# Cross-attention and quantised FFN on one core: the first two mixed tiles split ahead of the query turns, the x rows loaded ahead of the context blocks, row statistics and normalised rows one row tile sooner

## The chip, the cores and the metric

The kernel runs on one NeuronCore of a Trainium2 chip. The metric is device time in microseconds. Five engines work side by side and meet only at semaphores: TensorE (PE; its weight loads are shown as PEld), VectorE (DVE), ScalarE (ACT), GpSimd (POOL) and SyncE (SP), which here issues every DMA, in program order and on one queue. The granted clock of TensorE stands in the profile as a share of full speed: 1.00 is 2.4 GHz, 0.50 is 1.2 GHz.

## The reference

Eight batches of x (512 rows of 512) attend to a context of 512 rows of 512, then a quantised feed-forward net follows. Cut to what matters:

```
def attention(v, k, q, mask, W, b):          # v = k = context, q = layernorm(x)
    scores = einsum('bqd,bkd->bqk', q, k) / sqrt(512)
    att = softmax(where(mask, -1e9, scores))
    atted = swapaxes(einsum('bqk,bkd->bqd', att, v), -1, -2)
    return einsum('bdl,ol->bdo', atted, W) + b
def ffn(x, w_gate, w_up, w_down):            # weights: a scale per row; x and h: one scale each
    h = quant(silu(quant(x) @ quant(w_gate).T) * (quant(x) @ quant(w_up).T))
    return h @ quant(w_down).T
x = x + attention(context, context, layernorm(x), mask, W, b)
x = x + ffn(layernorm(x), ...)
```

One scale for the whole of x and one for the whole of h split the program into three stages with a full barrier between them: attention, gate and up products, down products.

## The kernel before

Everything the change touches is in the attention stage, in which batch n runs from 0 to 7. A 512x512 matrix is held as T = 4 row tiles of 128 partitions by 512 columns. To keep float32 accuracy each operand is held as a high and a low part (`_hi`, `_lo`), and each product is the sum of three matmuls; four column groups k of 12 matmuls make one 512x512 product.

TensorE's order in batch n is `scores(n, k)` (queries by context, k = 0 to 3), `merged(n-1, k)` (the last product of the batch before), `mixed(n, k)` (probabilities by W). All three write the same four PSUM tiles `mm[k]`. So `scores(n+1, k)` may start only when `mm[k]` has been read out: ACT copies it to `g_hi` (`mixed_hi`, L489), DVE makes `g_lo` (`mixed_lo`, L711), which raises `g_ready`. `scores(n+1, k)` also waits for `qT_ready`, the low part of the transposed queries.

The queries of batch n+1 go round a long way. DVE takes row statistics of x (`row_stats1`, L634 to L641), POOL the inverse deviation (`make_rstd1`, L385), DVE the bias (`row_bias1`, L656), ACT writes the normalised rows `qn` (`norm1`, L506). SP stores them to DRAM (`move_q`, L269), waits for the whole store, and loads them back in blocks as `qb` (L275). DVE turns each block (`turn_q`, L651), ACT makes `qT_hi` (`query_hi`, L471), POOL makes `qT_lo` (`query_lo`, L416). The context goes the same way without the store: `load_cb` (L261), `turn_c` (L646), `turned_hi` (L459), `turned_lo` (L410).

SP's DMAs in batch n, in order: transposes of the weights rounded in batch n-1 (`turn_w`, L300 and L304, after ACT's `weights16` L536 and L542), mask n+1 (L282), context rows n (L256), raw weights of batch n (L289, L294, after the transposes have landed), store and reload of the queries of n+1, store of the attention output of n-1 (`store_x1`, L309), context blocks n+2 (`load_cb`), then x of n+2 (`load_x`, L279). `load_x` waits for `x_free`, the landing of that very store, as the three x buffers take turns.

ACT ends a batch with `weights_round` (L524, L528) and `weights16`, which stand behind the four `g_hi`; DVE's `weights_scale` stands ahead of `turn_q`. POOL adds the merge bias to x (`add_bias`, L398). Nothing is scheduled by a planner: the order on each engine is the order of the loops below.

Of the kernel before, what the change touches and what calls it, by code (L numbers as in the profile page):

```python
# [48 lines left out]
def cross_attention_ffn(nc, x, context, mask, w_merge, b_merge, clip_x, clip_down,  # L49
                        w_gate, w_up, w_down, out):  # L50
    B, L, D = x.shape
    I = w_gate.shape[0]
    T = L // P
# [13 lines left out]
    with ExitStack() as whole:  # L67
# [19 lines left out]
        def attention():  # L87
            with ExitStack() as ctx:
# [165 lines left out]
                def _(sp):  # L254
# [23 lines left out]
                    def load_x(n):  # L278
                        sp.dma_start(xs[n % 3][:], x_t[n]).then_inc(x_in[n % 3], 16)  # L279
# [53 lines left out]
                    for n in range(B):  # L333
                        if n:
                            turn_w(n - 1)
                        if n < B - 1:
                            sp.wait_ge(mneg_made, T * (n + 1))
                            load_mask(n + 1)
                        if n:
                            sp.wait_ge(c_ready, T * n)  # L340
                            load_c(n)
                            sp.wait_ge(w_done, through(n - 1, w_turns))
                            load_w(n)
                            if n < B - 1:
                                move_q(n + 1)
                            for t in range(T):
                                store_x1(n - 1, t)
                        if n < B - 2:
                            sp.wait_ge(cT_ready, T * (n + 1))
                            load_cb(n + 2)  # L350
                            if n:
                                sp.wait_ge(min2, T * n)
                                sp.wait_ge(x_free[(n - 1) % 3], 64 * ((n - 1) // 3 + 1))
                            else:
                                sp.wait_ge(wm_done, T)
                            load_x(n + 2)
                        if n % 2:
                            store_scale(n)
                    sp.wait_ge(x_free[0], 64 * len(range(0, B, 3)))
# [10 lines left out]
                @block.gpsimd  # L370
                def _(gp):
                    def first_mneg(t):
                        if t == 0:
                            gp.wait_ge(mask_in, 16)
                        nc.gpsimd.tensor_scalar(mneg[:, t, :], mk[:, t, :], MASKED, None, ALU.mult).then_inc(mneg_made, 1)

                    def first_rstd(k):
                        a, b = FIRST_ROWS[k]
                        gp.wait_ge(var1, k + 1)
                        nc.gpsimd.tensor_tensor(rstd1[:, a:b], ve1[:, a:b], minus_half[:, a:b],  # L380
                                                ALU.pow).then_inc(rstd1_made, 1)

                    def make_rstd1(n):
                        gp.wait_ge(var1, 3 + n)
                        nc.gpsimd.tensor_tensor(rstd1[:], ve1[:], minus_half[:, 0:T], ALU.pow).then_inc(rstd1_made, 1)  # L385

                    def make_rstd2(a, b):
                        gp.wait_ge(var2, 1 if a == 0 else 2)
                        nc.gpsimd.tensor_tensor(ln2[:, a:b, 4 * T:5 * T], ve2[:, a:b, :],
                                                minus_half[:, 0:(b - a) * T].rearrange("p (b t) -> p b t", t=T),  # L390
                                                ALU.pow).then_inc(rstd2_made, 1)

                    def add_bias(n):
                        if n == 0:
                            gp.wait_ge(const_in, 48)
                        for t in range(T):
                            gp.wait_ge(q_ready, T * n + t + 1)
                            nc.gpsimd.tensor_tensor(xs[n % 3][:, t, :], xs[n % 3][:, t, :], bias[:],  # L398
                                                    ALU.add).then_inc(resid_ready, 1)

                    def make_c_lo(n):
                        gp.wait_ge(c_hid, n + 1)
                        for t in range(T):
                            nc.gpsimd.tensor_tensor(c_lo[:, t, :], cx[:, t, :], c_hi[:, t, :].bitcast(F32),  # L404
                                                    ALU.subtract).then_inc(c_ready, 1)

                    def turned_lo(n):
                        for t in range(T):
                            gp.wait_ge(cT_hid, T * (n - 1) + t + 1)
                            nc.gpsimd.tensor_tensor(columns(cT_lo, t), blocks(cb[:, t, :]), columns(cT_hi, t).bitcast(F32),  # L410
                                                    ALU.subtract).then_inc(cT_ready, 1)

                    def query_lo(n):
                        for t in range(T):
                            gp.wait_ge(qT_hid, T * (n - 2) + t + 1)
                            nc.gpsimd.tensor_tensor(columns(qT_lo, t), blocks(qb[:, t, :]), columns(qT_hi, t).bitcast(F32),  # L416
                                                    ALU.subtract).then_inc(qT_ready, 1)

                    nc.gpsimd.memset(minus_half[:], -0.5).then_inc(consts, 1)
                    nc.gpsimd.memset(ident[:], 0.0).then_inc(consts, 1)  # L420
                    gp.wait_ge(consts, 2)
                    nc.gpsimd.affine_select(out=ident[:], in_=ident[:], compare_op=ALU.not_equal, fill=1.0,
                                            base=0, pattern=[[-1, P]], channel_multiplier=1).then_inc(consts, 1)
                    gp.wait_ge(consts, 3)
                    nc.gpsimd.tensor_copy(ident16[:], ident[:]).then_inc(consts, 1)
                    first_rstd(0)
                    first_rstd(1)
                    first_mneg(0)
                    first_rstd(2)
                    for t in range(1, T):  # L430
                        first_mneg(t)
                    for n in range(B):
                        add_bias(n)
                        if n < B - 1:
                            make_rstd1(n + 1)
                            turned_lo(n + 1)
                            if n:
                                query_lo(n + 1)
                        make_c_lo(n)
                    make_rstd2(0, B - 1)  # L440
                    make_rstd2(B - 1, B)
# [3 lines left out]
                def _(act):  # L445
# [106 lines left out]
                    for n in range(B):  # L552
                        last, start = n == B - 1, n == 0
                        for t in range(T):
# [7 lines left out]
                            else:  # L562
                                if t < 2:
                                    make_mneg(n, t + 2)
                                if t:
                                    probs_hi(n, t - 1)
                        if not start:
                            if not last:
                                for t in range(T):
                                    norm1(n + 1, t)  # L570
                            probs_hi(n, T - 1)
                        if not last:
                            for t in range(T):
# [1 line left out]
                                if start:  # L575
                                    norm1(n + 1, t)
                        context_hi(n)
                        if not (start or last):
                            for t in range(T):
                                query_hi(n + 1, t)  # L580
                        for k in range(T):
                            mixed_hi(n, k)
                            if start:
                                for g in Q1_AFTER[k]:
                                    transposed_hi(n + 1, T + g)
                            if not last and k in (1, 2):
                                make_mneg(n + 1, k - 1)
# [9 lines left out]
                def _(dve):  # L597
# [184 lines left out]
                    for n in range(B):  # L782
                        last, start = n == B - 1, n == 0
                        for t in range(T):
                            mask_and_max(n, t)
                            if start:
# [4 lines left out]
                                invert_sum(n, t)  # L791
                                if t < 2:
                                    transposed_lo(0, T + 2 + t)
                            elif t:
                                invert_sum(n, t - 1)
                                if t < 3 and not last:
                                    row_stats1(n + 1, 2 * t - 2, 2 * t)
                                if t == 3 and not last:
                                    row_bias1(n + 1)
                                    for k in range(T // 2):  # L800
                                        turn_c(n + 1, k)
                                probs_lo(n, t - 1)
                        if start:
                            probs_lo(n, T - 1)
                            row_stats1(n + 1, 0, T)
# [12 lines left out]
                                row_stats2(n - 1, k)  # L818
                                row_min2(n - 1, k)
                        weights_scale(n)  # L820
                        if not (start or last):
                            for t in range(T):
                                turn_q(n + 1, t)
                        for k in range(T):
                            if start:
                                mixed_lo(n, k)
                                for g in Q1_AFTER[k]:
# [576 lines left out]
```

## Time and profile before

| | |
|---|---|
| median of 3 runs | 561.69 us (559.78 to 562.91) |
| the profiled execution's own time | 564.96 us |
| its span, first to last instruction | 562.9 us |
| attention stage | 0 to 317.3 us |
| PE busy | 526.2 us (93% of the span) |
| DVE, ACT, POOL busy | 416.4, 311.9, 168.3 us |
| mean granted clock | 0.979 |
| DMA queue, share of 16 engines | 65.7% |

The span is 2.1 us shorter than the profiled execution's own time, which includes what lies around the first and last instruction. The profiled execution is 3.3 us above the median of the timed runs. A busy share is a mean over stages; the stage with the change is read in laps, from the first score matmul of one batch to the first of the next.

### The profile page before, as it was taken

The numbers are of one execution on the slowest core, as the hardware profiler recorded it, in microseconds if no ns is written. First come the engines' busy times: TensorE is split into PE (matmuls) and PEld (weight loads), VectorE is DVE, ScalarE is ACT, GpSimd is POOL, SyncE is SP. The second block draws the span as 40 slices with busy tenths as digits, with TensorE's granted clock in tenths as the row PEclk, the third lists the DMA queues.
The fourth block names the chain that finished last, engine by engine and source line by source line (L and its number), as shares of the span: only waits on it lengthen the run. The fifth ranks groups of instructions, "written<-read, shape, count | busy, mean of one in ns | idle before, by whom it ended". The sixth has DMA issues, their size and how long they took to land. (4 is left out here: it accounts for less than half of the span.)

```text
span 562.9 us, 7193 instructions
## 1 busy us (share of the span) xinstructions
PE 526.2 (93%) x2344; PEld 341.0 (61%) x2344; DVE 416.4 (74%) x791; ACT 311.9 (55%) x456; POOL 168.3 (30%) x142
## 2 busy tenths in 40 slices
PE   5889979979999799896999899999999999999996
PEld 4678768858778588785888544444444444344442
DVE  5686886848868578586483767887787777599985
ACT  4758747477386564973723255455545543877520
POOL 3556347375494553953824000000000000000000
PEclk9989999989999799999999899999999999999999
DMA  8808796897978968996357554596421000779773
GB/s 273 231 3 176 266 236 153 252 245 241 233 173 263 242 203 221 215 268 151 78 167 95 174 172 164 164 318 234 123 71 37 19 19 4 305 270 399 259 276 150
DMA packets 93726, 106.17 MB, mean 189 GB/s; under 512 B 36864, under 2 KB 67584, under 8 KB 91136
## 3 DMA queue, kind: packets, MB, share of 16 engines
q1 hardware_dynamic: 93696, 105.80, 65.7%
q8 instruction: 16, 0.26, 0.2%
q14 instruction: 14, 0.11, 0.1%
HBM read 66.06 MB, written 31.72 MB: 174 GB/s over the span
## 5 line engine op out<-in xcount | busy, mean ns | idle before, releaser
L1325 PE MATMUL gu<-hid,gu_T 128*128 128x512 f16 x704 | 152.1, 379 | 0.0
L1325 PEld LDWEIGHTS gu<-hid,gu_T 128*128 128x128 f16 x704 | 68.8, 98 | 83.3 <-DVE hid L1240 0.4
L1143 ACT ACTIVATE hid<-gu,gu_mul 128x512 f32<-128x512 f32 x88 | 59.5, 685 | 73.6 <-PE gu L1325 68.0
L1221 DVE SCALAR_TENSOR_TENSOR hid<-gu,gu_mul,hid 128x512 f32 (+1 forms) x88 | 65.0, 746 | 33.4 <-PE gu L1325 29.5
L881 PE MATMUL mm<-cT_hi,qT_hi 128*128 128x512 f32 x128 | 54.4, 425 | 19.8 <-DVE g_lo L711 18.1
L1366 PE MATMUL gu<-wd_T,gu_T 128*128 128x512 f16 x264 | 58.0, 379 | 1.0 <-DVE gu_T L1266 0.9
L881 PE MATMUL mm<-wm_hi,p_hi 128*128 128x512 f32 x128 | 50.8, 397 | 4.0 <-DVE wm_lo L608 3.5
L1167 ACT ACTIVATE h<-hid,inv 128x512 int8<-128x512 f32 (+3 forms) x32 | 44.2, 1455 | 17.2 <-DVE gu_T L1266 13.4
L1229 DVE TENSOR_REDUCE hmax<-hid 128x1 f32 (+2 forms) x48 | 53.1, 1119 | 0.0
L883 PE MATMUL mm<-cT_hi,qT_lo 128*128 128x512 f32 x128 | 52.6, 411 | 0.0
L882 PE MATMUL mm<-cT_lo,qT_hi 128*128 128x512 f32 x128 | 52.4, 410 | 0.0
L882 PE MATMUL mm<-wm_lo,p_hi 128*128 128x512 f32 x128 | 50.6, 395 | 0.0
L883 PE MATMUL mm<-wm_hi,p_lo 128*128 128x512 f32 x128 | 50.6, 395 | 0.0
L881 PE MATMUL mm<-g_hi,c_hi 128*128 128x512 f32 x128 | 49.8, 389 | 0.0
L882 PE MATMUL mm<-g_lo,c_hi 128*128 128x512 f32 x128 | 49.8, 389 | 0.0
L883 PE MATMUL mm<-g_hi,c_lo 128*128 128x512 f32 x128 | 49.8, 389 | 0.0
L1111 POOL PARTITION_ALL_REDUCE top<-hmax x1 | 0.4, 381 | 162.5 <-DVE hmax L1253 162.5
L410 POOL TENSOR_TENSOR cT_lo<-cb,cT_hi 128x512 fp32r<-128x512 f32 x28 | 35.5, 1302 | 33.9 <-ACT cT_hi L459 33.8
L416 POOL TENSOR_TENSOR qT_lo<-qb,qT_hi 128x512 fp32r<-128x512 f32 x24 | 30.0, 1280 | 52.3 <-ACT qT_hi L471 52.3
L1366 PEld LDWEIGHTS gu<-wd_T,gu_T 128*128 128x128 f16 x264 | 25.5, 98 | 33.0 <-DVE gu_T L1266 2.8
L404 POOL TENSOR_TENSOR c_lo<-cx,c_hi 128x512 fp32r<-128x512 f32 x32 | 40.3, 1295 | 14.7 <-ACT c_hi L516 14.7
L881 PEld LDWEIGHTS mm<-cT_hi,qT_hi 128*128 128x128 f32 x128 | 25.9, 202 | 27.8 <-DVE g_lo L711 20.6
(145 smaller groups left out, 890.7 us busy)
## 6 DMA issues: line engine op xcount, KB each, us to landing
h_dram<-hid SPq DMA_DIRECT2D x3, 2816.0 KB, 9.3
hid<-h_dram SPq DMA_DIRECT2D x3, 2816.0 KB, 11.7
cb<-in_ctx_dram SPq DMA_DIRECT2D x28, 256.0 KB, 7.9
cx<-in_ctx_dram SPq DMA_DIRECT2D x7, 1024.0 KB, 6.4
q_dram<-qn SPq DMA_DIRECT2D x24, 256.0 KB, 5.2
qb<-q_dram SPq DMA_DIRECT2D x24, 256.0 KB, 5.2
x<-in_x_dram SPq DMA_DIRECT2D x5, 1024.0 KB, 8.4
x_dram<-x SPq DMA_DIRECT2D x20, 256.0 KB, 6.6
```

The lines of the kernel that those rows point to most:

```text
L404: nc.gpsimd.tensor_tensor(c_lo[:, t, :], cx[:, t, :], c_hi[:, t, :].bitcast(F32), ALU.subtract).then_inc(c_ready, 1)
L410: nc.gpsimd.tensor_tensor(columns(cT_lo, t), blocks(cb[:, t, :]), columns(cT_hi, t).bitcast(F32), ALU.subtract).then_inc(cT_ready, 1)
L416: nc.gpsimd.tensor_tensor(columns(qT_lo, t), blocks(qb[:, t, :]), columns(qT_hi, t).bitcast(F32), ALU.subtract).then_inc(qT_ready, 1)
L881: nc.tensor.matmul(bank[:], a_hi[:, t, cols], b_hi[:, t, :], start=t == 0, stop=False)
L882: nc.tensor.matmul(bank[:], a_hi[:, t, cols], b_lo[:, t, :], start=False, stop=False)
L883: last = nc.tensor.matmul(bank[:], a_lo[:, t, cols], b_hi[:, t, :], start=False, stop=t == T - 1)
L1143: nc.scalar.activation(silu[SILU_AT[i]], gu[2 * (i % 3)][:], ACT.Silu, scale=gu_mul[:, 0, i:i + 1]).then_inc(silu_done, 1)
L1167: nc.scalar.activation(h8[:, a:b, :].rearrange("p i l -> p (i l)"), hid[:, slot2(s), a * L:b * L], ACT.Copy, scale=inv[:, 1:2]).then_inc(h ...
L1221: nc.vector.scalar_tensor_tensor(hid[:, b % SLOTS, i * L:(i + 1) * L], gu[2 * (i % 3) + 1][:], gu_mul[:, 1, i:i + 1], silu[SILU_AT[i]], AL ...
L1229: nc.vector.tensor_reduce(hmax[:, k:k + 1], hid[:, b % SLOTS, lo * L:hi * L], AX_X, ALU.max, apply_absolute_value=True).then_inc(hmaxed, 1)
L1325: last = nc.tensor.matmul(gu[2 * (i % 3) + g][:], gu_T[:, g, h, i * P:(i + 1) * P], xT[p][:, h, :], start=h == 0, stop=h == T - 1)
L1366: last = nc.tensor.matmul(yb[T * (s % 2) + t][:], hq[s % 2][:, i, t * P:(t + 1) * P], wd_T[:, i, :], start=i == 0, stop=i == NI - 1)
```

## The change

Four things are moved, nothing is added or removed.

1. In batches 1 to 6, DVE's four `turn_q` and ACT's four `query_hi` move from ahead of the loop over the mixed tiles to between tiles 1 and 2 of it.
2. SP issues `load_x(n+2)` ahead of `load_cb(n+2)`, and with it moves the wait for `x_free`.
3. DVE takes the row statistics of batch n+1 at t = 0 and 1 in place of 1 and 2, and `row_bias1` at t = 2 in place of 3; ACT writes the normalised rows at t = 2 and 3, between the softmax tiles, in place of after them.
4. POOL does `make_rstd1(n+1)` ahead of `add_bias(n)` in batches 1 to 6.

```
@@ SP
                         if n < B - 2:
-                            sp.wait_ge(cT_ready, T * (n + 1))
-                            load_cb(n + 2)
                             if n:
                                 sp.wait_ge(min2, T * n)
                                 sp.wait_ge(x_free[(n - 1) % 3], 64 * ((n - 1) // 3 + 1))
...
                             load_x(n + 2)
+                            sp.wait_ge(cT_ready, T * (n + 1))
+                            load_cb(n + 2)
@@ POOL
-                        add_bias(n)
+                        if n == 0 or n == B - 1:
+                            add_bias(n)
                         if n < B - 1:
                             make_rstd1(n + 1)
+                            if n:
+                                add_bias(n)
@@ ACT
                                 if t:
                                     probs_hi(n, t - 1)
+                                if t >= 2 and not last:
+                                    norm1(n + 1, 2 * t - 4)
+                                    norm1(n + 1, 2 * t - 3)
                         if not start:
-                            if not last:
-                                for t in range(T):
-                                    norm1(n + 1, t)
                             probs_hi(n, T - 1)
@@ DVE
-                            elif t:
-                                invert_sum(n, t - 1)
-                                if t < 3 and not last:
-                                    row_stats1(n + 1, 2 * t - 2, 2 * t)
+                            else:
+                                if t:
+                                    invert_sum(n, t - 1)
+                                if t < 2 and not last:
+                                    row_stats1(n + 1, 2 * t, 2 * t + 2)
+                                if t == 2 and not last:
+                                    row_bias1(n + 1)
@@ ACT and DVE (query_hi on ACT, turn_q on DVE)
-                        if not (start or last):
-                            for t in range(T):
-                                query_hi(n + 1, t)
                         for k in range(T):
+                            if k == 2 and not (start or last):
+                                for t in range(T):
+                                    query_hi(n + 1, t)
                             mixed_hi(n, k)
```

The rows below are ACT's from the last context copy of batch 3 (`c_hi`) to the rounding of weights (`wst`), before:

```order
L516 ACTIVATE c_hi<-cx 128x2048
L471 ACTIVATE qT_hi<-qb 128x4x4x32 x4
L489 ACTIVATE g_hi<-mm 128x512 x2
L465 ACTIVATE mneg<-mk 128x512
L489 ACTIVATE g_hi<-mm 128x512
L465 ACTIVATE mneg<-mk 128x512
L489 ACTIVATE g_hi<-mm 128x512
L524 ACTIVATE wst<-wst,gu_inv 128x512 x2
```

and now:

```order
L519 ACTIVATE c_hi<-cx 128x2048
L492 ACTIVATE g_hi<-mm 128x512 x2
L468 ACTIVATE mneg<-mk 128x512
L474 ACTIVATE qT_hi<-qb 128x4x4x32 x4
L492 ACTIVATE g_hi<-mm 128x512
L468 ACTIVATE mneg<-mk 128x512
L492 ACTIVATE g_hi<-mm 128x512
L527 ACTIVATE wst<-wst,gu_inv 128x512 x2
```

Two of the four mixed tiles and one mask tile (`mneg`) now stand ahead of the query copies; DVE has the same move, two `g_lo` ahead of the four turns of `qb`.

SP's queue in batch 3, from the reload of the queries to the next weight transposes, before:

```order
L275 DMA qb<-q_dram 32x16x128 x4
L309 DMA x_dram<-x 128x512 x4
L261 DMA cb<-in_ctx_dram 32x16x128 x4
L279 DMA x<-in_x_dram 128x4x512
L316 DMA d_scale_dram<-d_step 128x1
L300 DMA_TRANSPOSE gu_T<-wst 128x4x128 x2
```

and now:

```order
L275 DMA qb<-q_dram 32x16x128 x4
L309 DMA x_dram<-x 128x512 x4
L279 DMA x<-in_x_dram 128x4x512
L261 DMA cb<-in_ctx_dram 32x16x128 x4
L316 DMA d_scale_dram<-d_step 128x1
L300 DMA_TRANSPOSE gu_T<-wst 128x4x128 x2
```

The context blocks (`cb`) change places with the x rows, and so stand behind the wait for `x_free` and next to the weight transposes.

## Rows read from the trace of the kernel before

**Rows 1.** Waits of PE in total: us in total, times, longest us.

```profile
PE mm L881 <- DVE g_lo L711: 18.1, 6, 4.4
```

**Rows 2.** One lap: busy us by engine, then PEclk, DMA share, GB/s.

```profile
155.74:192.45 36.71, 32.94 (x144) 26.96 (x144) 26.96 (x62) 23.36 (x39) 21.11 (x18) 0.98 0.88 226
```

**Rows 3.** Timeline of PE: start us, us, instruction, idle before and releaser.

```profile
81.48 0.50 PE L881 MATMUL mm<-cT_hi,qT_hi 128*128 128x512 f32 x1 [3.19 <-DVE g_lo L711]
155.74 0.50 PE L881 MATMUL mm<-cT_hi,qT_hi 128*128 128x512 f32 x1 [1.59 <-DVE g_lo L711]
266.73 0.79 PE L881 MATMUL mm<-cT_hi,qT_hi 128*128 128x512 f32 x1 [4.42 <-DVE g_lo L711]
```

**Rows 4.** Columns as in rows 2, the stretch behind the last such wait.

```profile
266.25:269.65 3.40, 2.92 (x7) 2.35 (x8) 2.69 (x8) 3.40 (x8) 3.40 (x4) 0.50 0.00 0
```

**Rows 5.** Timeline of DVE, 151 to 156 us.

```profile
151.32 2.49 DVE L651 STREAM_TRANSPOSE qb<-qb 128x512 f32<-128x512 f32 x4 [0.81 <-DMA qb<-q_dram]
155.00 1.29 DVE L711 TENSOR_TENSOR g_lo<-mm,g_hi 128x512 fp32r<-128x512 f32 x2 [1.18 <-ACT g_hi L489]
```

**Rows 6.** Timeline of ACT, 152 to 163 us.

```profile
152.07 2.41 ACT L471 ACTIVATE qT_hi<-qb 128x512 fp32r<-128x512 f32 x4 [6.79 <-DVE qb L651]
154.39 1.07 ACT L489 ACTIVATE g_hi<-mm 128x512 fp32r<-128x512 f32 x2
155.34 0.63 ACT L465 ACTIVATE mneg<-mk 128x512 bf16<-128x512 uint8 x1
155.86 0.60 ACT L489 ACTIVATE g_hi<-mm 128x512 fp32r<-128x512 f32 x1
...
157.34 1.35 ACT L524 ACTIVATE wst<-wst,gu_inv 128x512 int8<-128x512 f32 x2
```

**Rows 7.** Timeline of POOL, 152 to 158 us.

```profile
152.78 5.02 POOL L416 TENSOR_TENSOR qT_lo<-qb,qT_hi 128x512 fp32r<-128x512 f32 x4 [8.12 <-ACT qT_hi L471]
```

**Rows 8.** Timeline of SP's DMA issues, 143 to 183 us.

```profile
143.60 1.91 SPq L275 DMA_DIRECT2D qb<-q_dram  x4
145.55 2.79 SPq L309 DMA_DIRECT2D x_dram<-x  x4
148.39 3.45 SPq L261 DMA_DIRECT2D cb<-in_ctx_dram  x4
154.50 0.39 SPq L279 DMA_DIRECT2D x<-in_x_dram  x1
...
162.42 2.51 SPq L300 DMA_TRANSPOSE gu_T<-wst  x2
...
166.46 0.83 SPq L282 DMA_DIRECT2D mk<-in_mask_BxSxS_bk_dram  x1
...
169.74 0.37 SPq L289 DMA_DIRECT2D wst<-in_L_ffn_w_gate_dram  x1
...
172.06 2.79 SPq L269 DMA_DIRECT2D q_dram<-qn  x4
180.17 2.62 SPq L275 DMA_DIRECT2D qb<-q_dram  x4
```

**Rows 9.** Columns as in rows 2: the DMA engines within that lap.

```profile
161.50:163.50 2.00, 2.00 (x10) 1.65 (x10) 1.16 (x4) 2.00 (x5) 2.00 (x3) 1.00 0.09 27
168.00:178.50 10.50, 10.50 (x48) 8.71 (x47) 8.87 (x24) 7.62 (x14) 4.20 (x4) 1.00 0.95 314
```

**Rows 10.** DMA issues at 154.5, 278.0, 40.8 us: KB each, median us to landing.

```profile
x<-in_x_dram SPq DMA_DIRECT2D x1, 1024.0 KB, 8.4
...
cx<-in_ctx_dram SPq DMA_DIRECT2D x1, 1024.0 KB, 5.5
...
cb<-in_ctx_dram SPq DMA_DIRECT2D x4, 256.0 KB, 4.9
```

**Rows 11.** Transposes issued at 333 to 338, then at 352 to 358 us: us to landing.

```profile
hid<-hid SPq DMA_TRANSPOSE x4, 2.5
...
hid<-hid SPq DMA_TRANSPOSE x4, 5.4
```

More of the change, by code:

```diff
@@ L793, in _ @@
                                     transposed_lo(0, T + 2 + t)
-                            elif t:
-                                invert_sum(n, t - 1)
-                                if t < 3 and not last:
-                                    row_stats1(n + 1, 2 * t - 2, 2 * t)
+                            else:
[5 more added lines that the diff above has]
+                                    row_bias1(n + 1)
                                 if t == 3 and not last:
-                                    row_bias1(n + 1)
                                     for k in range(T // 2):
                                         turn_c(n + 1, k)
-                                probs_lo(n, t - 1)
+                                if t:
+                                    probs_lo(n, t - 1)
                         if start:
@@ L820, in _ @@
                         weights_scale(n)
-                        if not (start or last):
-                            for t in range(T):
-                                turn_q(n + 1, t)
                         for k in range(T):
+                            if k == 2 and not (start or last):
+                                for t in range(T):
+                                    turn_q(n + 1, t)
                             if start:
```

## The prediction

> **What bounds the kernel now.** I read first the waits of PE, then the laps, then the timelines of one lap engine by engine, and last the DMA issues. The chain of waits does not help: in the attention stage it follows PE's own matmuls. PE waits for `g_lo` six times, 18.1 us in all [rows 1], each time ahead of the first score matmul of batches 2 to 7; three of the six are shown, 3.19, 1.59 and 4.42 us [rows 3]. From 81.48 to 266.73 us there are five laps, 185.25 us or 37.05 each. PE's own work in a lap at full clock is 144 matmuls in 32.94 us [rows 2]. The rest is the wait and what the wait does to the clock: behind the last one the granted clock is 0.50 for 3.4 us [rows 4], which is the lower level, 1.2 GHz, and costs half of that stretch, 1.7 us.
>
> What is late? `g_lo` starts at 155.00 because ACT copies `g_hi` only behind the four `qT_hi`, and these wait for DVE's turns of `qb`, which wait for the reload of the queries [rows 5, 6]. From the start of the turns (151.32) to PE's start (155.74) are 4.42 us. The reload lands at the end of a closed loop, which I follow through batch 3 into 4: turns of `qb` at 151.32 [rows 5], weights rounded from 157.34 [rows 6], transposes of them issued at 162.42, mask at 166.46, raw weights at 169.74 once the transposes have landed, query stores from 172.06, their landing at 180.17 where the reload is issued [rows 8], then 7.86 us until the next turns at 188.03 (151.32 plus the lap of 36.71 us in rows 2; turn and PE start keep their 4.42 us in every lap). From 168.0 to 178.5 us the DMA engines are 0.95 busy at 314 GB/s [rows 9]. So this is a loop of DMA queue and engines, and PE is only its guest: an edit is worth what it takes off the loop, not what it takes off PE's wait.
>
> **Part 1, mixed tiles ahead of the turns.** Three things follow.
>
> (a) From turn to PE. `g_lo` of tiles 0 and 1 is now ready before the turns (their matmuls end over 5 us before those of tile 3), so `scores` waits for `qT_lo` of tile 0 instead. That is 0.75 us from the turn to ACT (152.07), 0.71 from ACT to POOL (152.78), one POOL operation of 5.02/4 = 1.26 [rows 5 to 7] and some 0.1: 2.8 us in place of 4.42. The gain is 1.6 us. It counts once, at the last lap, since in the laps before PE just waits for the loop. The later `qT_lo` come 1.26 us apart, against 2.73 us of matmuls for a tile, and cannot stall PE. `g_lo` of tiles 2 and 3, behind the query copies, is wanted 5.5 us after PE's start and is there after 2.
>
> (b) From turn to rounding. ACT has 157.34 - 151.32 = 6.02 us between them. Out of this stretch go two `g_hi` (154.39 to 155.34, 0.95) and one `mneg` (155.34 to 155.86, 0.52) [rows 6]. The weights are rounded 1.47 us sooner in the loop, at most 5 x 1.47 = 7.4 us over five laps.
>
> (c) The added cover: two `g_lo` ahead of the turns are 1.29 us of DVE [rows 5], but DVE sat idle 0.81 us ahead of the turns even in this lap, and part 3 makes it earlier. I take nothing, against 0.5 us a lap if it is wrong.
>
> **Part 2, x ahead of the context blocks.** `load_x` waits in any case until the output store has landed; SP was released from that at 154.50 [rows 8]. Before, 1 MB of context blocks filled the queue meanwhile, issued from 148.39. Now it is issued from about 154.9 on. x alone takes 5.5 us, as the lone 1 MB load does, instead of 8.4 [rows 10], so x lands 2.9 us earlier. The blocks come after it: a 256 KB piece lands 4.9 us after its issue when alone [rows 10], and four at the spacing of their issue (3.45 us for four) or of 1.4 us. x data ends near 158.5, so the last block lands near 165, where the queue had been empty by 162.9 (154.50 + 8.4); between 161.5 and 163.5 it was 0.09 busy [rows 9]. Nobody waits for the blocks themselves before the softmax tile t = 3, some 14 us after PE's start. But the weight transposes now want to start 1.47 us sooner, at about 161, while the queue stays full until 163.5 to 165. Transposes issued into a full queue exist in the feed-forward stage: 5.4 us to landing against 2.5 in a free one [rows 11]. So the price per lap is between nothing (four transposes are issued over 4 to 5 us, and can catch up) and 2.9 us. Nearest is the first end, since the backlog lasts only for the first half of the issues: I take 0.6 us a lap.
>
> The Trainium skill (DMA: Bandwidth & Descriptors, Queues, rings and completion order) says that each DMA engine consumes descriptors in ring order, with only one such queue for SyncE. By that the transposes stand behind all of the blocks and part 2 has a cost of its own; the trace agrees in that the raw weights, issued ahead of the query stores, are also served first. The same page (Latency and other measured facts) gives DMA transposes 261 GB/s: four of 128 KB would be an estimated 2.0 us, short enough to catch up. By that figure the price falls to the low end and the lap keeps nearly all of 1.47 us.
>
> **Part 3 and 4, statistics, normalised rows and `rstd` sooner.** `qn` is written some 2 to 3 us earlier, but its stores (172.06) already stood behind the raw weights (169.74) in a queue that was full until 178.5 [rows 8, 9]. So the queries land no earlier for it: I take 0, at most 0.3 us a lap. ACT's four normalisations no longer stand ahead of the last `p_hi`, which frees DVE earlier for the output rows; that only hides (c). `row_stats1` at t = 0 can stall DVE until x lands, about 5.5 us after PE's start, while the next score tile ends 5.8 after it: hidden. Without part 2 it would be 2.9 us later and not hidden. POOL's `add_bias`, 5 us, now waits for `rstd` and ends before `turned_lo` is due; what it makes is used a batch later.
>
> **The sum,** against the profiled execution's 564.96 us. Lap: 1.47 - 0.6 = 0.9 us; five laps 4.5. Last turn to PE 1.6. First lap (PE's wait of 3.19 us falls too, 0.2 us since the turns in batch 1 followed the landing late) 0.2. The clock behind the last wait: the wait shrinks from 4.42 towards 3 us; the row with 1.59 us kept the clock and those with 3.19 and 4.42 lost it, so I take 0.4 x 1.7 = 0.7. In all 7.0 us: 558.0 for a profiled execution. The timed runs have their median 3.3 us lower, at 561.69, so 554.7.
>
> **The rivals.**
>
> *The transposes catch up wholly.* Each lap gains 1.47: 7.4 + 1.6 + 0.2, and the last wait is short enough to keep the clock, 1.7: 10.9 us, 550.8. For it: they are issued 1.3 us apart and the backlog is short. Against: the issues themselves slow down in a full queue.
>
> *The loop does not move.* The price of part 2 eats the 1.47, and 1.6 to 2 us at the last lap remain: 559.9. For it: the queue was 0.95 busy, and the same bytes must pass.
>
> *Slower: the blocks hold up the weight transposes.* Place: SP's queue between `cb` and `gu_T`. All four transposes land 2.9 us later as in rows 11, mask, context, weights and queries follow them in the queue, and each lap grows by 2.9 - 1.47 = 1.4 us, five laps 7.1, less 1.6 at the end: 5.5 us slower, 567.2. It decides from a price above 1.8 us a lap, where 5 x (price - 1.47) exceeds 1.6. For it: the idle gap of the engines after the output store, while `load_x` is on its way, is no longer filled. Against: the 2 us at 161.5 that were idle before take most of it up.
>
> *All of the wait goes.* If early `qn` did shorten the loop to PE's 32.8 us, 18.1 us of waits and four more slow-clock stretches would go, some 26: about 536. Against it speaks all of rows 8 and 9.
>
> **How the numbers follow.** Forecast 0.50, catching up 0.20, loop unmoved 0.16, slower 0.10, all gone 0.04. A difference under 0.5% (2.8 us) can't be told from none here. Faster by more are the first, second and last, 0.74, and a little of the third: 0.76; slower 0.09; the same 0.15. The range is 549.5 to 563.5: it takes in the forecast with its price from nothing to 1.5 us a lap, the second case, the third, and leaves out the slower end and the last.
>
> **What would show it.** In the trace after, PE's start should follow the turn of `qb` by 2.8 us and wait for `qT_lo`, not `g_lo`. SP should issue x at the same distance behind the output stores, blocks right behind it; the first transposes should take over 2.5 us to land and the raw weights should be issued nearer to the mask. The query stores should be issued sooner and yet land right behind the raw weights. Laps near 36.1 us, with 1 to 3.5 us of wait in each. The prediction is wrong if laps come out at 35 or less (then early `qn` did shorten the loop), or above 37 (then the blocks cost more than the order saves).

## The result: 1.0% slower

| | before | after |
|---|---|---|
| median of 4 runs each, same chip | 560.93 us (559.78 to 562.91) | 566.71 us (564.76 to 568.76) |
| ratio, 95% interval | | 1.010 (1.005 to 1.015) |
| the profiled execution's own time | 564.96 us | 566.02 us |
| span | 562.9 us | 564.0 us |
| mean granted clock | 0.979 | 0.979 |

Forecast were 554.7 us and a range of 549.5 to 563.5, with 0.76 on faster. The time is 12 us above the forecast and outside the range. The two profiled executions differ by 1.1 us and the medians by 5.8, because the profiled execution of before ran 4.0 us above the median and that of after 0.7 below. So I use the traces for where the time goes, and timed ratios for how much; the other 4.7 us stand in no trace. Here and below a ratio compares the runs of the faster state alone and a median takes all runs, so the two can differ a little.

PE's waits, from the list of waits, name no engine any more ("issue" is idle time for which the profile shows no releaser). Columns: engine, tile, line, what released it, sum of the waits (us), count, longest (us).

```profile
PE mm L887 <- issue: 20.3, 5, 6.5
...
DVE qb L654 <- DMA qb<-q_dram: 20.7, 6, 6.6
```

The 18.1 us in six waits for `g_lo` [rows 1] are now 20.3 us in five, and DVE waits as long, for the reload of the queries. The first score matmuls of batches 4 and 5, in PE's timeline (start, duration, line, operation, in brackets the idle time before):

```profile
154.95 0.47 PE L887 MATMUL mm<-cT_hi,qT_hi 128*128 128x512 f32 x1 [0.15 <-issue]
...
194.34 0.77 PE L887 MATMUL mm<-cT_hi,qT_hi 128*128 128x512 f32 x1 [6.47 <-issue]
```

and DVE's turns ahead of them:

```profile
152.10 2.49 DVE L654 STREAM_TRANSPOSE qb<-qb 128x512 f32<-128x512 f32 x4 [1.38 <-DMA qb<-q_dram]
...
191.52 2.49 DVE L654 STREAM_TRANSPOSE qb<-qb 128x512 f32<-128x512 f32 x4 [6.58 <-DMA qb<-q_dram]
```

From turn to PE it is 2.85 and 2.82 us, against 4.42 [rows 3, 5]. POOL's four `qT_lo` start at 153.56 and take 5.06 us, so the first is done at about 154.83 and PE starts 0.12 us later. But PE waited hardly at all for the one and 6.47 us for the other: the laps now alternate. Between those turns lie 39.42 us, where before had 36.71 [rows 2]. That long lap as a window (columns as in [rows 2]) has the same 144 matmuls in it:

```profile
154.95:194.34 39.39, 32.92 (x144) 26.95 (x145) 27.41 (x61) 23.54 (x39) 21.14 (x18) 0.98 1.00 210
```

The same loop as in [rows 8], in SP's timeline of after:

```profile
155.13 0.38 SPq L279 DMA_DIRECT2D x<-in_x_dram  x1
155.56 2.99 SPq L261 DMA_DIRECT2D cb<-in_ctx_dram  x4
158.59 1.90 SPq L316 DMA_DIRECT2D d_scale_dram<-d_step  x1
...
161.70 3.00 SPq L300 DMA_TRANSPOSE gu_T<-wst  x2
...
164.75 2.35 SPq L304 DMA_TRANSPOSE wd_T<-wst  x1
...
167.14 0.58 SPq L282 DMA_DIRECT2D mk<-in_mask_BxSxS_bk_dram  x1
...
173.91 0.37 SPq L289 DMA_DIRECT2D wst<-in_L_ffn_w_gate_dram  x1
...
174.89 2.12 SPq L269 DMA_DIRECT2D q_dram<-qn  x4
...
184.11 1.91 SPq L275 DMA_DIRECT2D qb<-q_dram  x4
```

Here is the lap cut at these points, and summed over all five (batches 2 to 6), from the two timelines:

| us | before, this lap | after, this lap | before, five laps | after, five laps | difference |
|---|---|---|---|---|---|
| turn of `qb` to the issue of the first weight transpose | 11.10 | 9.60 | 54.4 | 46.9 | -7.4 |
| to raw weights (the transposes have landed) | 7.32 | 12.21 | 37.0 | 49.6 | +12.6 |
| to the reload of the queries | 10.43 | 10.20 | 56.0 | 53.8 | -2.2 |
| to the next turn | 7.86 | 7.41 | 37.9 | 36.8 | -1.1 |
| lap | 36.71 | 39.42 | 185.2 | 187.1 | +1.9 |

With the first turn 0.6 us later and the last path to PE 1.6 shorter that is +0.9 of the trace's +1.1 us. The gain in the first row is all there; the second row eats it and more. By batch (2, 3, 4, 5, 6) the second row reads 8.5, 6.4, 7.3, 6.3, 8.4 before and 12.3, 7.5, 12.2, 6.9, 10.7 after. The loss sits in the even batches. These carry two gate/up transposes and one of `w_down`, the odd ones four of gate/up. The DMA issues of an even lap (158 to 167 us) and of an odd one (125 to 132), with their median us to landing:

```profile
d_scale_dram<-d_step SPq DMA_DIRECT2D x1, 0.5 KB, 13.7
...
gu_T<-wst SPq DMA_TRANSPOSE x2, 9.6
...
wd_T<-wst SPq DMA_TRANSPOSE x1, 9.1
...
gu_T<-wst SPq DMA_TRANSPOSE x4, 4.4
```

And the engines in windows of that even lap, two wide ones, then the second cut into pieces of 1 us. The last two columns are the DMA engines' share and GB/s. The share counts the whole time of a packet in the window where it starts, so it can pass 1: after 4.59 follows 0.00.

```profile
164.00:167.50 3.50, 3.50 (x17) 2.92 (x16) 2.38 (x9) 2.02 (x6) 3.07 (x3) 1.00 1.46 168
...
167.50:171.50 4.00, 4.00 (x19) 3.30 (x19) 3.79 (x9) 3.92 (x7) 2.97 (x3) 1.00 1.43 44
...
167.00:168.00 1.00, 1.00 (x7) 0.81 (x6) 0.49 (x1) 1.00 (x2) 1.00 (x2) 1.00 4.59 223
168.00:169.00 1.00, 1.00 (x6) 0.84 (x5) 1.00 (x5) 0.92 (x3) 1.00 (x1) 1.00 0.00 0
169.00:170.00 1.00, 1.00 (x6) 0.84 (x5) 1.00 (x2) 1.00 (x3) 1.00 (x2) 1.00 0.11 2
170.00:171.00 1.00, 1.00 (x6) 0.81 (x5) 0.80 (x2) 1.00 (x3) 0.47 (x1) 1.00 1.15 79
```

From 167.5 to 171.5 us long packets are under way and next to nothing is moved: 44 GB/s, where a full queue moved 314 [rows 9], and from 168 to 170 no more than 2. It is the rate that shows this, not the share, which is 1.46 in the window before, where 168 GB/s pass. The prediction knew a queue that is full and passes bytes. This is a queue that is full and stalls.

### The profile page after: what moved, and what is told of

Same layout as the page of the kernel before. It is cut to its first block and busy times, and to the rows that moved or that the text cites. A ratio compares the mean times of both kernels' runs of the same rounds, so it can differ in the third digit from the quotient of the medians.

```text
span 564.0 us, 7193 instructions
## 1 busy us (share of the span) xinstructions
PE 524.8 (93%) x2344; PEld 340.7 (60%) x2344; DVE 420.5 (75%) x791; ACT 313.0 (55%) x456; POOL 169.4 (30%) x142
## 5 line engine op out<-in xcount | busy, mean ns | idle before, releaser
L887 PE MATMUL mm<-cT_hi,qT_hi 128*128 128x512 f32 x128 | 54.5, 426 | 22.0 <-issue 20.3
## 6 DMA issues: line engine op xcount, KB each, us to landing
hid<-h_dram SPq DMA_DIRECT2D x3, 2816.0 KB, 11.9
```

The lines of the kernel that those rows point to most:

```text
L887: nc.tensor.matmul(bank[:], a_hi[:, t, cols], b_hi[:, t, :], start=t == 0, stop=False)
```

## The experiments

Eighteen kernels ran. Each is compared with the kernel before on its own chip; "gap" is the second row of the table above, from the issue of the first weight transpose to that of the raw weights, for batches 2 to 6.

### Which part costs

Before with part 2 alone (e1), after without part 2 (e2), before with part 1 alone (e3), before with parts 3 and 4 alone (e4). The edit of e1, reversed in e2:

```
+                            (wait for x_free)
+                            load_x(n + 2)
                             sp.wait_ge(cT_ready, T * (n + 1))
                             load_cb(n + 2)
-                            (wait for x_free)
-                            load_x(n + 2)
```

e3 takes the two `k == 2` pieces of the diff of ACT and DVE, e4 all that is left.

e1: 

> Before with part 2 alone: x ahead of the context blocks on SP's queue. Theory A (the context blocks now stand next to the weight transposes and hold them up, most of all where the transpose of a w_down tile, 704 KB read, meets a full queue): slower than before by 5 to 9 us, as none of the savings is there to offset it; raw weights issued 2 to 4 us later in the lap in batches 2, 4 and 6, about 1 us later in 3 and 5. Theory B (the loss comes from the order on DVE and ACT, not from the queue): same as before within 1.5 us.

e2: 

> The changed kernel without part 2: context blocks ahead of x, as before; all the rest as changed. Theory A: faster than before by 3 to 9 us (five laps of up to 1.5 us, 1.6 us at the last), laps of 35.5 to 36.5 us, transposes land 2.5 us after their issue. Theory B: slower than before by 4 us or more, as the changed kernel is. In both, DVE's row statistics at t = 0 wait 1 to 3 us longer for x.

e3: 

> Before with part 1 alone: two mixed tiles ahead of the turns of the queries on DVE and ACT. Theory A: faster by 3 to 9 us, the same as the kernel with all but part 2 within 1.5 us; from turn to PE 2.8 us, weights rounded 1.5 us sooner after the turn. Theory B: slower, since two g_lo delay the turns.

e4: 

> Before with parts 3 and 4 alone: row statistics and normalised rows one tile sooner, POOL's rstd ahead of the bias. Theory A and the prediction: same as before within 1 us, since the query stores stand behind the raw weights in the queue. If the loop were held by the normalised rows, it would be faster by 0.5 to 2 us a lap, 3 to 10 in all. Theory B with the statistics as the cause (DVE stalls for x at t = 0): slower by 3 us or more.

| kernel | median us (before 564.58) | ratio, interval | gap by batch |
|---|---|---|---|
| e1 part 2 | 571.60 | 1.013 (1.008 to 1.017) | 11.3, 7.1, 10.3, 6.3, 9.4 |
| e2 parts 1, 3, 4 | 560.27 | 0.987 (0.981 to 0.994) | 9.4, 8.1, 7.1, 6.3, 8.3 |
| e3 part 1 | 556.47 | 0.987 (0.983 to 0.992) | 8.7, 7.0, 8.2, 6.4, 6.2 |
| e4 parts 3, 4 | 565.86 | 1.003 (0.999 to 1.006) | 8.4, 6.7, 6.9, 6.3, 7.1 |

Part 2 alone costs 1.3%, part 1 alone gives 1.3%, parts 3 and 4 do nothing. e2 is the least sure of the four: its runs spread from 553.1 to 563.0 us, and the two medians alone would give 0.992. Turn to first transpose is 9.6 or 9.05 us in every kernel with part 1 and 11.1 or 10.55 in every one without. PE's waits with part 1 alone, on its waits page:

```profile
PE mm L881 <- issue: 10.5, 6, 2.8
```

### Only where the small store stands

Part 2 in batches 0, 2, 4 alone (e5: `if n % 2 == 0:` around the new order, the old one otherwise) and in 1, 3, 5 alone (e6). Behind an odd n come `store_scale(n)` and then the mixed set of transposes.

e5: 

> Before, with x ahead of the context blocks only in batches 0, 2 and 4, behind which SP transposes four gate and up tiles. Theory A1 (the price arises where the transpose of a w_down tile meets a full queue): within 1.5 us of before. Theory A2 (any transposes behind the blocks pay by the delay of the queue, about the same in each lap): about half of the 7.1 us that the full swap cost, less what batch 0 gives, 2.5 to 4 us slower.

e6: 

> Before, with x ahead of the context blocks only in batches 1, 3 and 5, behind which SP transposes two gate and up tiles and one w_down tile. Theory A1: 5 to 8 us slower than before, as much as the full swap; first transpose to raw weights 10 us or more in batches 2, 4 and 6, 6.3 us in 3 and 5. Theory A2: 3.5 to 5 us slower.

e5 ran in 563.49 us, e6 in 568.65, with 561.74 for before: 1.003 (1.001 to 1.006) and 1.010 (1.007 to 1.013). Of e6 the gaps are 9.6, 6.4, 9.5, 6.3, 8.8; of e5 8.5, 6.4, 6.9, 6.4, 6.2. So three of the six swaps carry most of the cost, those of the even laps. Both results lie a little beside what was expected: e5 1.75 us above before instead of 1.5 at most, the gaps of e6 under 10 us. Two things are special there: the transpose of `w_down`, and the store of its scales, 512 bytes, in 128 pieces of 4 (one number from each partition), ahead of the transposes.

### Are the copies behind the transposes to blame?

e7 is after, with the mask and the context rows held back until the transposes have landed:

```
 if n:
     turn_w(n - 1)
+    sp.wait_ge(w_done, through(n - 1, w_turns))
```

> The changed kernel, with SP holding the mask and context loads back until the weight transposes have landed. Theory C (the copies queued behind the w_down transpose collide with it): first transpose to its landing falls from 10.7 to 12.3 us to 8 or less in batches 2, 4 and 6; the raw weights go out that much sooner, and the total falls by 2 to 6 us although mask and context rows start later. Theory D (the collision is with the context blocks ahead of the transposes): the time to landing stays above 10 us in these batches and the total rises by 2 to 6 us.

576.15 us, 1.024 (1.021 to 1.028). First transpose to landing is still 11.3, 7.5, 11.6, 6.6, 9.8. The window behind the transposes, with nothing issued after them:

```profile
171.00:174.00 3.00, 3.00 (x15) 2.49 (x14) 2.76 (x7) 2.92 (x7) 3.00 (x3) 1.00 1.40 23
```

The same stall (23 GB/s). What holds it stands ahead of or in the transposes. The extra 1.4% over after (1.024 by 1.010, measured on two chips) I put down to loads issued later; nothing tests that. In time it is 8 us, more than the 2 to 6 expected.

### Is it the long transpose of `w_down`?

e10 is after and e11 before, with that transpose of 11 column blocks in three DMAs of 4, 4 and 3 (`DOWN_PARTS`); e14 is after, with `w_down` transposed ahead of the two of gate/up.

```
-sp.dma_start_transpose(wd_T[:, :, r * P:(r + 1) * P], cols)
+for lo, hi in DOWN_PARTS:
+    sp.dma_start_transpose(wd_T[:, lo:hi, r * P:(r + 1) * P], cols[:, lo * P:hi * P])
```

e10: 

> The changed kernel with each w_down tile transposed by three DMAs (4, 4 and 3 of its 11 column tiles) in place of one. Theory F1 (the stall is that of one long transpose, 1408 columns, in a full queue; four of 512 columns passed a full queue without it): from the first transpose to the raw weights in batches 2, 4 and 6 falls from 10.7 to 12.3 us to 8 to 9, and the total falls by 3 to 6 us to that of before. Theory F2 (any 704 KB of transposes of this tile behind the context blocks stall): above 10 us as now, and the total stays or rises by up to 2 us.

e11: 

> Before with the same split of the w_down transposes, the control for the split itself. Under both theories two more DMA issues of about 1.3 us in three laps: 0 to 4 us slower than before, less where a stall goes that before has in batch 6 (8.4 us from the first transpose to the raw weights, of which 4.3 us are issue).

e14: 

> The changed kernel with the w_down tile transposed ahead of the gate and up tiles. G1: unchanged within 2 us, the scale store still stands in front. G2: the stall moves with the w_down transpose; the time from the first transpose to the last landing changes by 2 us or more in batches 2, 4 and 6, in either direction.

e10 was 568.69 us, 1.012 (1.008 to 1.017), with gaps of 12.3, 8.3, 11.9, 6.9, 12.1: no better than after, so the theory that the long transpose stalls the queue fell. It is the gaps that say so; the time alone could not, since splitting has a price of its own (e11). (The 704 KB in the expectation is the tile's size in float32; as the transpose takes it, in 2-byte numbers, it has 352 KB.) e14 was 568.23, 1.008 (1.005 to 1.012); its gaps are 12.6, 7.4, 12.0, 6.6, 11.4 us. Its lap in SP's timeline:

```profile
157.60 2.08 SPq L316 DMA_DIRECT2D d_scale_dram<-d_step  x1
...
161.07 3.89 SPq L300 DMA_TRANSPOSE wd_T<-wst  x1
...
165.01 2.93 SPq L304 DMA_TRANSPOSE gu_T<-wst  x2
...
173.08 0.37 SPq L289 DMA_DIRECT2D wst<-in_L_ffn_w_gate_dram  x1
```

12.0 us from 161.07 to 173.08: whichever goes first, all of them are late. e11 was a miss: I expected 0 to 4 us over before and it cost 8.7, 1.016 (1.013 to 1.019), with the stretch from raw weights to reload up from 11.3, 11.3, 10.4, 12.6, 10.4 to 11.9, 10.8, 13.1, 11.7, 12.0. Why splitting costs so much is open; each of the new DMAs has its own issue on SP.

### The store of the scales

The four stores of `w_down` scales move from the loop to the end of the attention stage, where nothing but the last output stores stands ahead of them (in e13 the engines move 132 GB/s from 284 to 286 us, then next to nothing until 290). Nobody reads them before the last stage.

```
-                        if n % 2:
-                            store_scale(n)
+                    for n in range(1, B, 2):
+                        store_scale(n)
```

e13 is after with it, e15 is e3 with it, e17 is before with it, e18 is e1 with it.

e13: 

> The changed kernel, with the four stores of the w_down scales (512 bytes each, 4 bytes a partition) moved to the end of the attention stage. Theory G1 (the scale store, queued straight ahead of the transposes, stalls the DMA engines): first transpose to landing falls from 10.7 to 12.3 us to 7 to 8.5 in batches 2, 4 and 6, the total falls by 5 to 10 us, below before. Theory G2 (it is the transpose of the w_down tile itself behind a full queue): 10 us or more as now, total unchanged within 1.5 us.

e15: 

> Before with part 1 alone and the scale stores at the end of the stage. G1: 0 to 4 us faster than part 1 alone (0.9873 of before), so 0.980 to 0.987; first transpose to landing 6.2 to 7 us in batches 4 and 6, where part 1 alone had 8.2 and 6.2. G2: the same ratio, within 0.003.

e17: 

> Before with the scale stores at the end of the stage and nothing else. G1: before has 7.3 to 8.5 us from first transpose to landing in batches 2, 4 and 6 with some stall in them; 0 to 3 us faster, 0.995 to 1.000 of before. If the store cost the old order as much as the new one: 5 us faster or more.

e18: 

> The same with x ahead of the context blocks. G1 alone: within 1.5 us of the kernel without the swap (0.995 to 1.002 of before), where with the store in its old place the swap cost 1.28%. If the queue itself has a price besides the stall (blocks land later, transposes delayed): 2 to 4 us above the kernel without the swap.

| kernel | median us | before us | ratio, interval | gap by batch |
|---|---|---|---|---|
| e13 after, stores at the end | 554.99 | 562.76 | 0.983 (0.979 to 0.988) | 7.6, 8.2, 7.7, 6.5, 6.9 |
| e15 part 1, stores at the end | 555.79 | 562.76 | 0.984 (0.980 to 0.989) | 7.0, 7.3, 6.5, 6.4, 6.2 |
| e17 before, stores at the end | 561.47 | 565.08 | 0.994 (0.991 to 0.997) | 6.7, 6.5, 6.2, 6.4, 6.2 |
| e18 part 2, stores at the end | 561.50 | 565.08 | 0.993 (0.990 to 0.996) | 6.8, 7.3, 6.2, 6.4, 6.2 |

This is the answer. With the 512 bytes out of the way part 2 costs nothing: e18 against e17, and e13 against e15, lie within each other's intervals. In place, it costs 1.3% (e1). Only the blocks' own share is left in the gaps: 0.2 us a lap more in e18 than in e17, and 0.7 more in e13 than in e15, which also differ in parts 3 and 4. e17 was expected at 0.995 to 1.000 and gained more. The same lap in SP's timeline of e1, then of e18:

```profile
165.60 2.51 SPq L300 DMA_TRANSPOSE gu_T<-wst  x2
...
175.91 0.37 SPq L289 DMA_DIRECT2D wst<-in_L_ffn_w_gate_dram  x1
```

```profile
163.07 2.50 SPq L300 DMA_TRANSPOSE gu_T<-wst  x2
...
169.26 0.37 SPq L289 DMA_DIRECT2D wst<-in_L_ffn_w_gate_dram  x1
```

10.31 us between them in the one, 6.19 in the other. SP's timeline of e13 in batch 4:

```profile
153.90 0.38 SPq L279 DMA_DIRECT2D x<-in_x_dram  x1
154.33 2.56 SPq L261 DMA_DIRECT2D cb<-in_ctx_dram  x4
...
160.95 3.18 SPq L300 DMA_TRANSPOSE gu_T<-wst  x2
...
164.18 1.46 SPq L304 DMA_TRANSPOSE wd_T<-wst  x1
...
168.60 0.37 SPq L289 DMA_DIRECT2D wst<-in_L_ffn_w_gate_dram  x1
```

The DMA issues of that stretch, us to landing, and the DMA engines in a window of it:

```profile
gu_T<-wst SPq DMA_TRANSPOSE x2, 4.6
...
wd_T<-wst SPq DMA_TRANSPOSE x1, 4.4
```

```profile
162.00:166.00 4.00, 4.00 (x19) 3.31 (x18) 3.81 (x15) 2.29 (x6) 2.59 (x3) 1.00 1.36 171
```

x, blocks and transposes stand as in after, the blocks are under way when the transposes are issued, and yet these land 4.4 to 4.6 us after their issue instead of 9.1 to 9.6 (in all even laps 4.4 to 5.6 instead of 7.5 to 10.7). The 171 GB/s are the rate that after has too until 167.5 us; what has no counterpart here is the stretch that follows it: cut into pieces of 1 us, this lap of e13 moves no less than 119 GB/s from 156 to 169 us. A short stall there is in e13 as well, in batch 3, with 6 GB/s from 128 to 129 us, so the store isn't the only thing that can make one. In e18, without part 1:

```profile
gu_T<-wst SPq DMA_TRANSPOSE x2, 3.2
...
wd_T<-wst SPq DMA_TRANSPOSE x1, 3.6
```

The store costs even in the kernel before, 0.6% (e17): there it was issued at 154.94 and landed after 12.2 us, but 7.5 us, not 3.1, lay between its issue and the first transpose. Slow it is wherever it stands: 12.2 to 14.3 us to landing in the loop of before and after, 8.8 to 10.2 at the end of the stage (e13).

### Does the order of the query stores matter?

SP issues the query stores ahead of the wait for the transposes and of the raw weights, in e2 (e8) and in e3 (e9); e12 is e8 with the split of e10; e16 is e8 with the scale stores at the end.

```
+                            store_q(n + 1)
                             sp.wait_ge(w_done, through(n - 1, w_turns))
                             load_w(n)
-                            move_q(n + 1)      # stores, waits, reloads
+                            move_q(n + 1)      # waits, reloads
```

e8: 

> The changed kernel without part 2, and SP stores the normalised rows ahead of the wait for the transposes and the raw weights (0.75 to 1.2 MB less ahead of the queries in the queue). If the loop is what the prediction says, turn to turn through the queue: the query store lands 2 to 3.5 us sooner after PE's start, laps of 33.5 to 35 us near PE's own 32.8, and the total is 8 to 14 us below before, 3 to 8 below the same kernel without this move; here the early rows do count. If the loop is held elsewhere (raw weights late for DVE's weights_scale): no faster than the kernel without this move, 553 to 557 against 560 to 565 of before.

e9: 

> Before with part 1 alone (late statistics and rows, as before), and SP stores the normalised rows ahead of the raw weights. If the early rows count once the queries no longer stand behind the raw weights: 1 to 4 us above the same kernel with early rows (0.9857 of before), so 0.988 to 0.993 of before, and the raw weights, which now wait for the late rows, go out 2 to 3 us later. If the early rows count for nothing anywhere: the same ratio within 0.003.

e12: 

> The changed kernel without part 2, with the query stores ahead of the raw weights and the w_down transposes split: the best that the theory gives. F1: as fast as without the split or up to 3 us faster, 551 to 556. F2: up to 4 us slower than without the split.

e16: 

> The changed kernel without part 2, query stores ahead of the raw weights (0.9857 of before), and the scale stores at the end of the stage. G1: 1 to 4 us faster than without the move, 0.979 to 0.985 of before, the fastest of all. G2: the same ratio.

| kernel | median us | before us | ratio, interval |
|---|---|---|---|
| e8 parts 1, 3, 4, stores first | 554.88 | 561.74 | 0.986 (0.982 to 0.989) |
| e9 part 1, stores first | 556.71 | 562.04 | 0.991 (0.987 to 0.995) |
| e12 e8, `w_down` in three DMAs | 559.98 | 562.04 | 0.995 (0.992 to 0.997) |
| e16 e8, scale stores at the end | 554.26 | 562.76 | 0.981 (0.975 to 0.987) |

SP in e8, one lap:

```profile
169.83 3.87 SPq L269 DMA_DIRECT2D q_dram<-qn  x4
173.74 0.45 SPq L291 DMA_DIRECT2D wst<-in_L_ffn_w_gate_dram  x1
...
175.61 1.93 SPq L277 DMA_DIRECT2D qb<-q_dram  x4
```

The stores no longer stand behind the raw weights, and the reload follows 5.8 us after the first store instead of 8.1 [rows 8]. Now early `qn` may count a little (e8 against e9; the intervals touch, so it isn't shown). Beside the kernels with the old order the stores first bring nothing that can be told: e8 has 0.986 and e2 0.987, e9 0.991 and e3 0.987. The raw weights are now issued behind the stores, so they come later. e12 confirms that splitting costs. e16 has the lowest ratio of all, 1.9% below before; e13 and e15 overlap with it. e16's waits of PE are 12.8 us in six:

```profile
PE mm L891 <- issue: 12.8, 6, 2.9
```

## Why the prediction was wrong, step by step

- **The loop bounds the stage: right.** In the profiled executions, the five laps sum to 187.1 us or more in every kernel at a ratio of 1.008 and above, and to 182.7 or less in every one at 0.995 and below.
- **Part 1, turn to PE 2.8 us instead of 4.42: right** (2.85 and 2.82, and PE starts 0.12 us behind the first `qT_lo`; the trace names no `g_lo` any more).
- **Part 1, weights rounded 1.47 us sooner: right** (-7.44 us over five laps against -7.35). In e3 part 1 brought 1.3% of time, 7 us, where (a) and (b) sum to 9.0; in its trace the five laps are 7.9 us shorter than in before, and the first turn comes 2.6 us later, for a cause not looked into.
- **Parts 3 and 4 nothing: right** (e4, 1.003, interval 0.999 to 1.006).
- **Part 2, 0.6 us a lap: this is the step that failed.** The working said that the four transposes "can catch up". They do in the odd laps (+1.1 and +0.5 us), but in the three even laps the gap grew by 3.8, 4.9 and 2.3 us; all five make 12.6 against 3.0 forecast. Of that, 3.3 us came back in the two stretches from the raw weights to the next turn, for which the sum had no term. The bound of 2.9 us a lap came from transposes behind a store of 2816 KB and a load of 1 MB [rows 11], and no row of those has a store of 4-byte pieces ahead of it. The price of the blocks was judged rightly, 0.2 to 0.7 us a lap in the gaps and nothing in the time (e18, e13), and x landed 5.4 us after its issue, as said; only the last block came at about 167 us in place of 165. What was missed is the `store_scale` that follows them, which stands in the order of SP's instructions and had no term because it is 0.5 KB.
- **Rival, slower: right place, near number, wrong reason.** It put the price between `cb` and `gu_T` and said 567.2 us; measured 566.71. But it blamed the 1 MB of blocks, for every lap; they hardly hold the transposes up (e18), and the laps alternate. The agreement of the number is partly chance: it added 2.9 us to five laps, the kernel adds 10.9 in three and 1.6 in two.
- **The clock: wrong sign.** I counted 0.7 us back at the last wait. That wait came out at 5.29 us, and the granted clock stood at 0.50 from 264.40 to 271.23 us, 6.8 us against 3.4 [rows 4]. PE sat idle in the first 3.24 us of them, so 3.59 us of its work ran at the lower clock. In before it was 2.90 us (the stretch of 3.4 began 0.5 us ahead of PE's start), which at half speed cost 1.45 us and not 1.7. Ahead of that wait lies batch 6's gap, 10.7 us against 8.4.
- **The start: 0.2 us to be gained.** The first turn came 0.6 us later instead.

What is shown and what isn't: shown is that store plus swap together make the large cost (before, e1, e17 and e18 are the four kernels with and without each), and that copies behind it (e7), the length (e10) and the order (e14) of the transposes don't make it. Not shown is what happens inside the DMA engines. How much the distance counts isn't shown by itself either: from the store to the first transpose are 6.9 to 7.5 us in before, where the store cost 0.6%, 5.0 to 5.5 in e1, where the swap cost 1.3% more, and 3.1 to 4.0 in after. But e2, without the swap, has 5.2 in batch 2 and a gap of 9.4, where e1 has 5.1 and 11.3: the blocks right ahead of the store count too. No run put another small transfer in the store's place. The Trainium skill (DMA: Bandwidth & Descriptors, Specifications) says that transfers under 512 bytes are done as read-modify-write; the pieces here have 4 bytes. Whether that is what makes 512 bytes take 13.7 us no run shows, as none varied the size of the pieces. The same page (Queues, rings and completion order) has each engine consume its descriptors in ring order; e14 agrees in so far as both kinds of transposes behind the store are late, in whichever order.

## What to carry to other kernels

In a loop that closes through one DMA queue, price every DMA in the row, by the form of its pieces and not by its bytes alone: 512 bytes in 4-byte pieces cost more here (0.6% in before, some 2.7% in after) than moving 1 MB of blocks next to the transposes (nothing that can be told). Before moving a large transfer, read what small one ends up between it and the next that somebody waits for, and put results that nobody reads yet where the queue is idle. A price taken from rows of a full queue holds only for a queue that is full of the same things.

## What the runs showed of the hardware

- A 512-byte store of 128 pieces behind 2 MB of loads took 13.7 us to land (batch 4 of after), and the DMA transposes behind it 9.1 to 9.6 us instead of 4.4 to 4.6 (e13), with 44 GB/s moved over 4 us.
- Four such stores at the end of the stage landed 8.8 to 10.2 us after issue (e13).
- In even laps, transposes behind 1 MB of blocks, without that store, landed 3.2 to 5.6 us after issue (e18, e13); without blocks or store right ahead it was 2.5 and 3.6 us (e17, batch 4).
- One transpose of 11 column blocks cut in three made the kernel 1.6% slower (e11, interval 1.3 to 1.9%), and e12 stands at 0.995 where e8 has 0.986, a difference of about 0.9%.
- Holding back the mask and context loads until the transposes have landed (e7) stands at 1.024 where after has 1.010: about 1.4%, as much as the swap itself.
